# Two of three segment sums: the one-hot matrices move from VectorE to ScalarE

## What is computed

```
# first block, twice: neighbours' mean, then a dense layer
neigh = x[col];  agg = segment_sum(neigh, row, n)
deg = max(segment_sum(ones, row, n), 1)
h = (x + agg / deg) @ W.T + b          # layer norm, silu
# second block: 8 experts, top 2 of them for each node, gelu between two matmuls
# third block: the same edges the other way round, with a weight for each edge
gathered = edge_weight[:, None] * node_states[edge_src]
aggregate = segment_sum(gathered, edge_dst, n)
# fourth block: a dense layer on the half of the nodes with the largest router weights
```

## Time and profile before

| | us |
|---|---|
| median of 3 runs | 7308.46 (7308.11 to 7312.75) |
| time of the profiled execution | 7351.86 |
| its span, first to last instruction | 7349.8 |
| POOL busy in the span | 3773.9 (51%) |
| PE busy | 3665.0 (50%) |
| DVE busy | 2691.0 (37%) |
| ACT busy | 911.7 (12%) |

### The profile page before, as it was taken

How to read it: one execution, slowest core, us unless ns; L and a number is a source line. 1 busy time by engine, 2 the same in 40 slices (tenths; PEclk the granted TensorE clock), 3 DMA queues, 4 the chain that set the end, 5 groups by cost and what they waited for, 6 DMA issues and landing times. The chain is left out here.

```text
span 7349.8 us, 62474 instructions
## 1 busy us (share of the span) xinstructions
PE 3665.0 (50%) x13987; PEld 2653.6 (36%) x13988; DVE 2691.0 (37%) x6479; ACT 911.7 (12%) x2424; POOL 3773.9 (51%) x3797
## 2 busy tenths in 40 slices
PE   4113965444444444445441222289992455565629
PEld 1001543333333333333230100078882333343517
DVE  5106854444334444444360000011113455555661
ACT  0001940000003000000230000022221100000322
POOL 4772036666663666666427777700005566666321
PEclk7556977777777777777655555599996677778859
DMA  3001113333312333332012000022214333333250
GB/s 135 1 0 35 15 54 92 92 90 91 92 52 62 93 91 91 90 91 84 19 41 71 1 4 4 9 71 75 88 57 130 90 89 90 89 91 91 70 161 18
DMA packets 290145, 497.57 MB, mean 68 GB/s; under 512 B 99253, under 2 KB 182880, under 8 KB 290048
## 3 DMA queue, kind: packets, MB, share of 16 engines
q0 software_dynamic: 163264, 345.19, 16.6%
q1 hardware_dynamic: 125696, 150.28, 6.3%
q10 hardware_dynamic: 1088, 1.05, 0.1%
HBM read 487.50 MB, written 92.89 MB: 79 GB/s over the span
## 5 line engine op out<-in xcount | busy, mean ns | idle before, releaser
L970 PE MATMUL sum_sums<-sum_got,sum_onehot 128*128 x4992 | 1612.1, 483 | 1709.3 <-DVE acc L1132 1340.8
L902 POOL DMA_INDIRECT sum_got<-xn,edge_row x1568 | 1537.7, 981 | 1169.3 <-issue 456.9
L970 PEld LDWEIGHTS sum_sums<-sum_got,sum_onehot 128*128 128x128 f32 x4992 | 1164.2, 243 | 2141.2 <-issue 1937.3
L1132 DVE TENSOR_TENSOR acc<-acc,sum_sums 128x257 f32 (+1 forms) x2496 | 1052.5, 422 | 1813.0 <-remote 1215.4
L902 POOL DMA_INDIRECT sum_got<-h,edge_row x784 | 754.7, 963 | 464.8 <-issue 223.0
L1270 POOL DMA_INDIRECT table<-rec,addr x784 | 810.4, 1034 | 300.2 <-issue 278.9
L1815 PE MATMUL moe_f_ps_y<-xb,moe_f_hT 128*128 128x256 f32 x1792 | 477.7, 399 | 313.2 <-issue 313.2
L1799 PE MATMUL moe_f_ps_h<-moe_f_xT,xb 128*128 128x256 f32 x1792 | 475.1, 398 | 304.2 <-issue 304.2
L1880 DVE TENSOR_TENSOR moe_f_y<-moe_f_ps_y,moe_b 128x256 f32<-128x256 f32 x112 | 42.2, 419 | 1368.4 <-PE moe_f_ps_y L1815 649.7
L1647 POOL DMA_INDIRECT moe_out_c_got<-moe_out,place_i x98 | 94.9, 968 | 824.9 <-PEq L1605 787.5
L1270 POOL DMA_INDIRECT table<-sort_rec,sort_addr x392 | 401.3, 1024 | 199.0 <-issue 121.6
(11 more groups left out here) (465 smaller groups left out, 3395.3 us busy)
## 6 DMA issues: line engine op xcount, KB each, us to landing
xb<-in_L_ffn_W SPq DMA_DIRECT2D x112, 1024.0 KB
sum_got<-xn,edge_row POOLq DMA_INDIRECT x1568
moe_in<-acc SPq DMA_DIRECT2D x28, 512.0 KB
moe_f_xin<-moe_in SPq DMA_DIRECT2D x56, 256.0 KB
moe_out<-moe_f_y SPq DMA_DIRECT2D x56, 256.0 KB
xn<-xb SPq DMA_DIRECT2D x14, 896.0 KB
table<-rec,addr POOLq DMA_INDIRECT x784
sum_got<-h,edge_row POOLq DMA_INDIRECT x784
```

The source lines that it names most:

```text
L902: pool.indirect_dma_start(got[:, c % SU, 0:D], None, source, bass.IndirectOffsetOnAxis(ap=p.edge_row[:, c:c + 1], axis=0)).then_inc(s_got[ ...
L970: mm = nc.tensor.matmul(sums[k % 2][j], onehot[:, (k % QUARTERS) * HALF + j, :], flat(got[:, bass.ds(where[n % PLAN], 1), :]), start=True, ...
L1132: v.tensor_tensor(a, a, sums[k % 2][j], ALU.add).then_inc(s_added[j], 1)
```

## The change

ScalarE gets a function that makes the four one-hots of a turn with five activations. For each of the four pieces it computes |row - column number| into a new buffer `distance` (Abs with scale -1 and the row as bias), waits for the four, and then takes relu(1 - distance) over all 512 columns at once, which is 1 where the two agree and 0 elsewhere. Before it, it waits for `s_sum` of the turn whose buffer it overwrites, and for its own last `s_onehot`. VectorE builds one-hots in sum2 alone. In sum0 the first four turns' one-hots are made between two of the clears and the last clear of `acc`.

```
+        distance = None if weighted else p.sb("distance", [P, HALF, P], F32, ctx)
...
         @block.scalar
         def _(act):
+            def hot(k, c, made):
+                if not isinstance(made, int) or made > 0:
+                    gate(act, s_onehot, made, s_turned_over)
+                for j in range(HALF):
+                    nc.scalar.activation(distance[:, j, :], p.iota[:], ACT.Abs, bias=p.edge_local[:, bass.ds(c + j, 1)],
+                                         scale=-1.0).then_inc(s_distance, 1)
+                act.wait_ge(s_distance, made * HALF + HALF)
+                nc.scalar.activation(onehot[:, k * HALF:(k + 1) * HALF, :], distance[:], ACT.Relu, bias=p.ones[:, 0:1],
+                                     scale=-1.0).then_inc(s_onehot, 1)
...
                 act.wait_ge(s_placed, 1)
+                if not weighted:
+                    for k in range(QUARTERS):
+                        hot(k, k * HALF, k)
                 clear(early, at)
+            elif not weighted:
+                for k in range(QUARTERS):
+                    hot(k, k * HALF, k)
...
+            if not weighted:
+                with act.Fori(0, PIECES // PLAN) as g:
+                    for k in range(QUARTERS):
+                        turn = act.snap(QUARTERS * g + k + 1)
+                        gate(act, s_sum, turn, s_turned_over)
+                        hot(k, PLAN * (g + 1) + k * HALF, act.snap(QUARTERS * (g + 1) + k))
...
-            for k in range(QUARTERS):
-                build(k, k * HALF, k + 1)
+            if weighted:
+                for k in range(QUARTERS):
+                    build(k, k * HALF, k + 1)
...
                         v.tensor_tensor(a, a, sums[k % 2][j], ALU.add).then_inc(s_added[j], 1)
-                    build(k, PLAN * (g + 1) + k * HALF, QUARTERS * (g + 1) + k + 1)
+                    if weighted:
+                        build(k, PLAN * (g + 1) + k * HALF, QUARTERS * (g + 1) + k + 1)
```

More of the change, by code:

```diff
@@ L754, in sum_over_edges @@
         s_landed, s_free = s("s_landed"), s("s_free")
+        s_distance, s_turned_over = s("s_distance"), s("s_turned_over")
         if centre:
@@ L1087, in build @@
                 number = p.iota[:].unsqueeze(1).to_broadcast([P, HALF, P])
[L1088 to L1095, removed]
+                local, weight = (row[:, bass.ds(c, HALF)].unsqueeze(2).to_broadcast([P, HALF, P])
+                                 for row in (p.edge_local, p.edge_weight))
+                v.tensor_tensor(out, number, local, ALU.is_equal).then_inc(s_built, 1)
+                dve.wait_ge(s_built, built)
+                v.tensor_tensor(out, out, weight, ALU.mult).then_inc(s_onehot, 1)
             if weighted:
```

## The result

The median is 7323.35 us after and 7308.46 before: a ratio of 1.0019, 95% interval 1.0012 to 1.0027. The time lies inside the predicted range, but on the wrong side of 1: +15 to +20 us where -16 was forecast, at the edge of what counts as a difference or just beyond it.

What follows compares the result with a forecast made beforehand. POOL's waits for late news of finished matmuls were taken as the bound. From the profiled 7351.86 us, - 14 (POOL) - 3 (ends) + 1 (semaphores) gave 7336, or 7292 for the median, lying 43.4 lower; range 7265 to 7340 us.

Steps and rivals of the forecast that it cites:

- What bounds the kernel: In sum0 and sum1 no engine is full; POOL waits for free slots, as news of finished matmuls comes only when it stops.
- the waits would stay near 50 in a sum: Expected sign in sum0 and sum1: POOL's waits for SP keep their number, near 50 each, and grow a little.
- POOL slowed by builds: Gathers of sum0 and sum1 run longer beside VectorE's builds; removing these takes 26 us off POOL.
- What of it reaches the time: Share of POOL's 26 us that shortens sum0 and sum1: 0.53, taken from sum2, so 14 us gained, bounds 0 and 26.
- 3 us at the ends of the sums: At the ends of sum0 and sum1 VectorE's last builds go: 1.5 us a sum gained, bounds 0 and 4.
- absorbed: Rival: POOL's saving in sum0 and sum1 goes wholly into its waits; 7305 us, chance 0.27.
- New semaphore traffic: ScalarE's seven posts a turn in sum0 and sum1, where VectorE posted one: cost 0 to 1 us, upper bound 28.
- the semaphores themselves: Rival: more posts and ScalarE work slow every gather as in sum2; +28 us, 7336 us, chance 0.13.
- ScalarE's own wait: Rival: ScalarE's distance posts come late, so TensorE waits for the Relu each round; +125 us, 7433 us, chance 0.09.
- The start of sum0: First one-hots go ahead of ScalarE's clear, moving the first adds from 1022.5 to about 1033; cost 0, bound 10 us.
- The chances: Odds for the whole kernel's time: faster 0.40, same 0.36, slower 0.24.

Runs made afterwards that it cites:

- neither: Kernel before without VectorE's builds in the turns of sum0 and sum1, first four one-hot groups reused, none made by ScalarE: 0.9989, 6 us under before.
- after_again: The changed kernel, unchanged, run again on the second chip: 1.0029 of before.
- before_again: The kernel before, unchanged, run again on the first chip (median 7342 us): 0.9997.
- before_third: The kernel before, unchanged, run on the third chip (median 7330 us): 1.0000.
- increments_only: Kernel before plus ScalarE's seven waits and increments a turn as plain semaphore instructions, no activations: 1.0022, 17 us over before.
- activations_only: Kernel before plus five ScalarE activations a turn into scratch tiles, with one increment a turn: 1.0023, 16 us over before.
- traffic: Kernel before plus all of the change's ScalarE work into scratch tiles, TensorE still using VectorE's one-hots: 1.0029, 22 us over before.
- fewer_instructions: Changed kernel with two ScalarE increments a turn and the rows of 16 pieces copied once to a fixed place: 1.0032, 25 us over before.
- fewer_posts: Changed kernel with two ScalarE increments a turn instead of seven, same five activations: 1.0013, 12 us over before.
- increments_19: Kernel before plus nineteen plain ScalarE semaphore increments a turn, no activations: 1.0316, 231 us over before.

## Why the prediction was wrong

- **What bounds the kernel** was right: POOL waits for news that comes when it has stopped, and the gather spans above differ by POOL's busy time and, against it, the wait for SP. That the waits would stay near 50 in a sum was wrong: there are 58.
- **POOL slowed by builds** was right: the gathers fell from 965 to 946 ns, and `neither`, too, has 948. The Trainium skill ("SBUF — State Buffer", section "Who interferes with whom") has it that an instruction of VectorE with two inputs in SBUF contends with one of GpSimd that reads SBUF; the 965 and 946 ns agree with that.
- **What of it reaches the time** was mis-sized. The prediction took a share of 0.53 of 26 us from sum2, 14 us, and 3 us at the ends of the sums. `neither` has the whole gain without ScalarE: 6 us (interval 1 to 15). In its two gather spans 22.6 us of busy time went and 3.6 came through, a share of 0.16. So sum2's pace was no price for its longer gathers alone; what else slows it was not tested. The 3 us at the ends did not show: the last add ends 22.4 and 22.3 us behind the start of the last gather in `after_again`, against 24.0 and 20.1 in the trace before, 20.0 and 15.2 in `before_again` and 19.9 and 19.6 in `before_third`. The rival "absorbed" (7305) described this part.
- **New semaphore traffic** is the step that failed: "I take 0 to 1", with 28 as the bound. The increments and waits alone cost 17 us (`increments_only`). The sum had no term at all for the activations themselves, and they cost 16 us with a single increment a turn (`activations_only`). Both together cost 22 us. The argument for 0 was that sum2's slower pace was already explained by its longer gathers. By the share of 0.16 these explain some 6 of the 18 ns a gather, an estimate, so it was not. The rival "the semaphores themselves" had the sign, though it put the cost into every gather; the gathers are not longer (965 ns in `traffic` as before), and POOL stops more often (58 times a sum).
- **ScalarE's own wait** (+125 us) did not come: with VectorE's one-hots in use (`traffic`) the cost is the same as with ScalarE's. ScalarE's 2.23 us a turn, where 3.1 were predicted, were short enough.
- **The start of sum0** was right. The first adds stand at 1033.48 in the trace after (1033 predicted), the next at 1038.27, and giving the first groups back to VectorE changes nothing.
- **The chances**: 0.24 for slower was too little. The gain and the two prices were all of a size that the traces bounded and did not settle, and the sum leaned on the favourable end of both.

That the measured time lies inside the range is owed to the rivals that the range took in, and not to the sum: its gain was nearly three times too large and its price missing. What stays open: by which way ScalarE's work costs POOL time, more stops in `traffic` and the changed kernel, longer ones in `fewer_instructions`. That activations do so with a single increment a turn is shown, and so is that increments alone do; what the two share is not. The slow steps of SyncE's own instructions, on which POOL's news depends, are in the kernel before as well, and do not grow in step with the cost: from 2450 to 3400 us, 36 of 405 take 0.6 to 0.76 us in `before_again` and 35 of 394 in `traffic`, 31 of 402 in `before_third` and 56 of 402 in `fewer_posts`.

## What to carry to other kernels

An engine that is idle is not free. Where the pace is set by how soon a semaphore's news gets to the engine that issues gathers, seven increments a turn on an idle engine, with their waits, cost more (17 us, 22 with the five activations) than 285 us of work taken off VectorE gave (6 us). Before moving work to an idle engine, count its increments and activations per round of the bounding loop, and price them by running them into a scratch tile on top of the kernel as it is: here one such kernel settled the sign. Take no share from a stage that differs in more than the one thing.

## What was not expected of the hardware

Late in a run of back-to-back indirect gathers, instructions of ScalarE's and SyncE's streams went on in steps of 1.4 us, increments and register instructions alike (`increments_19`, 2613 to 2623 us). Behind the last gather ScalarE's went on in steps of 0.07 us, and early in such a run most of them did so, too. The profile does not show what holds them. The same 1.4 us stand between ScalarE's instructions at the start of sum0, in the kernel with VectorE's first groups:

```profile
1024.83 0.20 ACT L872 ACTIVATION_READ_ACCUMULATOR row_L_gnn_b_self<-row_L_gnn_b_self 128x1 f32 x1 [0.99 <-issue]
1026.22 0.42 ACT L872 ACTIVATE row_L_gnn_b_msg<-row_L_gnn_b_msg 128x256 f32<-128x256 f32 x1 [1.19 <-issue]
1027.63 0.20 ACT L872 ACTIVATION_READ_ACCUMULATOR row_L_gnn_b_msg<-row_L_gnn_b_msg 128x1 f32 x1 [0.99 <-issue]
```

Idle time of ScalarE that nothing in the profile ends ("issue"), in steps of 1.4 us beside gathers, may be the same thing. And the same kernel differs by up to 45 us in its median between comparisons on different chips, three times the effect studied here; without runs of before on the same chip nothing of this could have been told.
